# A four-stage mixture-of-experts kernel: slot logits in steps of one PSUM bank, the third stage's batch end in two single banks, bias parts in later entries, and new instruction orders

## What is computed

```python
x = x + L0_ffn(L0_cond(x, cond))   # attention with gated experts, then an 8-expert MoE
x = x + L1_ffn(L1_cond(x, cond))   # one chosen expert MLP, then routed experts and a layernorm
x = x + L2_ffn(L2_cond(x, cond))   # two chosen skill MLPs and a shared one, then a soft MoE
x = x + L3_ffn(L3_cond(x, cond))   # masked linear mix, 16-head attention, shared and routed experts
```

```python
logits = (einsum('tzd,ed->tze', x, phi_w) + phi_b).reshape(t, z, n, p)
D = softmax(logits, axis=3); C = softmax(logits, axis=2)
X = clip(einsum('tznp,tzd->npd', D, x)); X = tanh(normalise(X))
Y = einsum('npd,ndH->npH', X, expert_w) + expert_b
out = einsum('tznp,npH->tzH', C, Y)
```

## Time and profile before

| | us |
|---|---|
| median of 3 runs | 1338.59 (1337.62 to 1344.19) |
| profiled execution | 1348.07 |
| its span, first to last instruction | 1346.3 |
| TensorE busy in it | 1107.3 |
| VectorE busy | 749.8 |
| ScalarE busy | 448.1 |
| GpSimd busy | 176.7 |
| mean granted TensorE clock | 0.897 of full speed |

### The profile page before, as it was taken

How to read it: one execution, slowest core, us unless ns; L and a number is a source line. 1 busy time by engine, 2 the same in 40 slices (tenths; PEclk the granted TensorE clock), 3 DMA queues, 4 the chain that set the end, 5 groups by cost and what they waited for, 6 DMA issues and landing times.

```text
span 1346.3 us, 17637 instructions
## 1 busy us (share of the span) xinstructions
PE 1107.3 (82%) x6726; PEld 784.2 (58%) x6726; DVE 749.8 (56%) x1645; ACT 448.1 (33%) x712; POOL 176.7 (13%) x170
## 2 busy tenths in 40 slices
PE   1358999999758999999898866579889898898775
PEld 0247888888645566567565434456556565665543
DVE  3245555655373556766666775264574755747533
ACT  1113545443441323343233211214333343333231
POOL 0982001110010000000000100112020120201100
PEclk8578999999877989999999886789999999999887
DMA  9000000000020121012100000300000000000000
GB/s 317 1 1 1 13 13 13 13 13 13 1 94 0 47 110 48 1 47 110 48 0 1 0 0 1 95 1 1 5 1 5 0 5 5 1 5 1 4 5 4
DMA packets 12890, 35.21 MB, mean 26 GB/s; under 512 B 3552, under 2 KB 7296, under 8 KB 12035
## 3 DMA queue, kind: packets, MB, share of 16 engines
q1 hardware_dynamic: 12486, 32.63, 6.9%
q10 hardware_dynamic: 288, 1.44, 0.3%
q0 software_dynamic: 32, 0.01, 0.0%
HBM read 33.02 MB, written 1.05 MB: 25 GB/s over the span
## 4 chain that ended last, share of the span: by engine, by line
PE 56%; issue 16%; DVE 13%; POOLq 4%; DVEq 4%; ACT 3%; POOL 2%; SPq 1%; DMA 1%; ACTq 0%
PE ps L1079 5%; PE ps L983 4%; PE ps L1009 4%; PE ps L1213 3%; PE ps L961 3%; PE ps L798 3%; PE ps L954 3%; PE ps L946 3%; PE ps L1067 3%; PE ps L808 2%; PE ps L1140 2%; DVE arena L1867 2%; PE ps L1156 2%; PE ps L844 2%; PE ps L832 1%
## 5 line engine op out<-in xcount | busy, mean ns | idle before, releaser
L1867 DVE TENSOR_REDUCE arena<-ps 128x8 f32<-128x2048 f32 x32 | 73.2, 2288 | 31.9 <-PE ps L1120 31.7
L1418 ACT ACTIVATE arena<-ps 128x2048 f32<-128x2048 f32 x32 | 60.1, 1879 | 84.0 <-PE ps L1144 84.0
L983 PE MATMUL ps<-arena,uR 128*128 128x512 f32 x128 | 76.8, 684 | 4.7 <-ACT arena L1364 4.7
L1009 PE MATMUL ps<-arena 128*128 128x128 f32 x512 | 70.9, 296 | 11.8 <-DVE xacc L1789 8.1
L1009 PEld LDWEIGHTS ps<-arena 128*128 128x128 f32 x512 | 66.1, 208 | 19.0 <-DVE xacc L1789 10.7
L1067 PE MATMUL ps<-uR,arena 128*128 128x256 f32 x256 | 74.5, 387 | 0.7 <-ACT arena L1391 0.7
L1079 PE MATMUL ps<-arena 128*128 128x256 f32 x256 | 63.5, 397 | 5.2 <-DVE arena L1848 3.7
L1213 PE MATMUL ps<-arena 128*128 128x512 f32 x128 | 62.4, 632 | 3.4 <-DVE yT L1934 2.0
L1391 ACT ACTIVATE arena<-ps 128x512 f32<-128x512 f32 x64 | 38.3, 598 | 75.5 <-PE ps L1068 66.5
L798 PE MATMUL ps<-arena 128*128 128x256 f32 x256 | 59.7, 392 | 2.6 <-DVE arena L1616 2.6
L954 PE MATMUL ps<-x2R,arena 128*128 128x256 f32 x192 | 54.0, 404 | 9.3 <-DVE arena L1757 9.1
(11 more groups left out here) (372 smaller groups left out, 2325.1 us busy)
## 6 DMA issues: line engine op xcount, KB each, us to landing
arena<-in_skills SPq DMA_DIRECT2D x16, 768.0 KB, 5.7
arena<-in_expert_w SPq DMA_DIRECT2D x2, 2048.0 KB, 8.0
arena<-in_l_experts SPq DMA_DIRECT2D x8, 386.5 KB, 3.2
arena<-in_consts_b ACTq DMA_DIRECT2D x1, 1408.0 KB, 8.3
x2R<-in_x SPq DMA_DIRECT2D x8, 128.0 KB, 2.5
arena<-in_L_w SPq DMA_DIRECT2D x2, 512.0 KB, 8.9
arena<-in_phiC SPq DMA_DIRECT2D x1, 1024.0 KB
arena<-in_expert_b SPq DMA_DIRECT2D x1, 1024.0 KB, 5.0
```

The lines of the kernel that those rows point to most:

```text
L983: mm(o, uR[:, b, k * P:(k + 1) * P], phiC[:, col:col + 512], start=True, stop=False)
L1009: last = mm(high[:, 2, t * P:(t + 1) * P], eD[h][:, k, col:col + P], uT[u][:, k, :], start=k == 0, stop=k == 1)
L1418: av(pexp[:, t, gp].rearrange("p c h t -> p (c h t)"), scores[:, :, :].rearrange("p c t -> p (c t)"), ACT.Exp, scale=SCALE3).then_inc(s.sc ...
L1867: V.tensor_reduce(nm[:, k, :, 2 * gp:2 * gp + 2], scores[:, :, :].rearrange("p c (h t) -> p c h t", h=2), X, ALU.max, negate=True).then_in ...
```

## The change

1. Each slot step covers one bank: 8 steps in place of 4 for LG, MT and SH on TensorE, ScalarE and (LG) VectorE. Step n+1 has its own bank; only step n+2 waits for the exponential of step n. The parts of the maxima have two buffers, padded to the same transposition. The sum, inverse and scaling on VectorE and XT stay at four.
2. In the third stage AV0 to G3 use bank 2 alone, and FF to OUT use bank 3 alone. AV0 waits for the gate read (G3A) of the batch before and no longer for its output. AV1 waits for AV0's copy; AVT and SA are two steps each; FF and FH four; RT and RM four.
3. PH is three steps (PHA, PHB, PHC) with the same three operations, and they, PX, W and WA stand later in GpSimd's list.
4. All lists are written anew.

```diff
-    PH.0 RA0.0 PH.1 PX.0 RG0.0 PH.2 PH.3 W.0 WA.0 RA0.1 W.1 WA.1 W.2 WA.2 W.3 WA.3 RG0.1 W.4 WA.4 W.5 WA.5 W.6
+    RA0.0 RG0.0 RA0.1 RG0.1 PHA.0 PHB.0 PHC.0 PHA.1 PHB.1 RA0.2 PHC.1 RA1.0 PHA.2 PHB.2 PHC.2 PHA.3 PHB.3 RG1.0
+    PHC.3 W.0 RG0.2 WA.0 PX.0 W.1 RA1.1 WA.1 W.2 WA.2 RA0.3 RG1.1 W.3 WA.3 W.4 WA.4 W.5 WA.5 W.6 RG0.3 WA.6 W.7
...
-    MT0.5 SG1.7 SH0.5 SU1.7 SG2.7 SU2.7 LG1.5 SG3.7 SG4.7 MT1.5 SG5.7 SH1.5 SU3.7 SU4.7 LG2.5 XT0.5 MT2.5 SU5.7
-    SH2.5 XT1.5 LG3.5 UC.7 MT3.5 CL2.0 SH3.5 CL3.0 MC.5 CL4.0 LG0.6 CL5.0 XT2.5 CL6.0 MT0.6 CL7.0 XT3.5 SH0.6
+    SU4.7 LG4.6 MT3.6 SU5.7 SH3.6 MT4.6 LG5.6 SH4.6 UC.7 MT5.6 LG6.6 SH5.6 UT.7 XT0.6 MT6.6 LG7.6 SH6.6 CL2.0
+    LG0.7 XT1.6 MT7.6 CL3.0 MC.6 SH7.6 CL4.0 MT0.7 CL5.0 LG1.7 SH0.7 CL6.0 LG2.7 CL7.0 MT1.7 XT2.6 SH1.7 MT2.7
...
-    TS1.7 RT1.6 TS2.7 TS3.7 OUT.6 AV0.7 AV1.7 AVT.7 SAT.7 WO.7 X5T.7 G3.7 FF0.7 FF1.7 SO.7 RT0.7 RT1.7 OUT.7""",
+    TS2.7 AV0.7 OUT.5 TS3.7 FF0.6 AV1.7 FF1.6 AVT0.7 AVT1.7 FF2.6 SAT.7 WO.7 FF3.6 SO.6 RT0.6 X5T.7 RT1.6 G3.7
+    RT2.6 RT3.6 OUT.6 FF0.7 FF1.7 FF2.7 FF3.7 SO.7 RT0.7 RT1.7 RT2.7 RT3.7 OUT.7""",
```

The slot steps on TensorE:

```diff
-                        else:
-                            pe.wait_ge(s.eD_ready, at(b, 4, st_ - 1))
-                        for c in range(2):
-                            o = high[:, c, :]
-                            col = h * HALF + c * 512
-                            mm(o, uR[:, b, k * P:(k + 1) * P], phiC[:, col:col + 512], start=True, stop=False)
-                            last = mm(o, con("ones3"), phib3[:, col:col + 512], start=False, stop=True)
-                        last.then_inc(s.lg_mm, 1)
+                        else:
+                            pe.wait_ge(s.eD_ready, at(b, 8, st_ - 2))
+                        col = h * HALF + c * 512
+                        mm(high[:, c, :], uR[:, b, k * P:(k + 1) * P], phiC[:, col:col + 512], start=True, stop=False)
+                        mm(high[:, c, :], con("ones3"), phib3[:, col:col + 512], start=False, stop=True).then_inc(s.lg_mm, 1)
```

The waits and steps of the third stage's batch end on TensorE:

```diff
                         if b > 0:
-                            pe.wait_ge(s.out_ready, at(b - 1))
+                            pe.wait_ge(s.g3_read, at(b - 1))
+                    else:
+                        pe.wait_ge(s.av_read, at(b, 2, 0))
...
-                if n in ("FF0", "FF1"):
...
+                for q in range(4):
+                    if n == f"FF{q}":
+                        v, j = q // 2, q % 2
+                        if q == 0:
+                            pe.wait_ge(s.x5C_ready, at(b))
+                            if b > 0:
+                                pe.wait_ge(s.out_ready, at(b - 1))
+                        else:
+                            pe.wait_ge(s.ffh_ready, at(b, 4, q - 1))
+                        w = (wsi, w1s)[v]
+                        mm(low[:, 3, 0:T], w[:, j, :], x5C[:, :], start=True, stop=True)
+                        mm(low[:, 3, T:2 * T], w[:, 2 + j, :], x5C[:, :], start=True, stop=True).then_inc(s.ff_mm, 1)
...
+                for r in range(4):
+                    if n == f"RT{r}":
+                        k, c = r // 2, r % 2
+                        if r == 0:
+                            pe.wait_ge(s.y2_ready, at(b))
+                        else:
+                            pe.wait_ge(s.rt_read, at(b, 4, r - 1))
```

More of the change, by code:

```diff
@@ L149 @@
+    PHC.3 W.0 RG0.2 WA.0 PX.0 W.1 RA1.1 WA.1 W.2 WA.2 RA0.3 RG1.1 W.3 WA.3 W.4 WA.4 W.5 WA.5 W.6 RG0.3 WA.6 W.7
+    WA.7 RA0.4 RA1.2 RG0.4 RG1.2 RA1.3 RA0.5 RG1.3 RG0.5 RA0.6 RA1.4 RG1.4 RG0.6 RA1.5 RA0.7 RG1.5 RG0.7 RA1.6
+    RG1.6 RA1.7 RG1.7""",
 }
@@ L540, in build @@
         phib_h = w3y[0:3].rearrange("p b d -> p (b d)")[:, 0:HALF // 2].bitcast(BF16)
-        nmd = tb([P, 32])
-        nmd3 = tb([P, P], BF16)
-        mdT = tb([64, P], BF16)
+        nmd = tb([P, 16])
+        nmd3 = [tb([P, P], BF16) for _ in range(2)]
+        mdT = [tb([64, P], BF16) for _ in range(2)]
         dsum = tb([P, 32])
-        nmc = tb([P, K, 2, 32])
+        nmc = tb([P, K, 4, 32])
+        mcn = tb([P, K, 32])
         mc3 = tb([P, K, P], BF16)
@@ L968, in step_b @@
                     last.then_inc(s.uC_T, 1)
-                for st_ in range(4):
-                    h, k = st_ // 2, st_ % 2
+                for st_ in range(8):
+                    h, k, c = st_ // 4, st_ // 2 % 2, st_ % 2
                     if n == f"LG{st_}":
-                        if st_ == 0:
+                        if st_ < 2:
                             pe.wait_ge(s.uC_ready, at(b))
@@ L991, in step_b @@
                     if n == f"SH{st_}":
-                        pe.wait_ge(s.mdT_ready, at(b, 4, st_))
-                        pe.wait_ge(s.lg_read, at(b, 4, st_))
-                        for c in range(2):
-                            last = mm(high[:, c, :], mdT, selD[:, c * 512:(c + 1) * 512],
-                                      start=False, stop=True, skip_group_check=True)
-                        last.then_inc(s.lg_shift, 1)
+                        pe.wait_ge(s.mdT_ready, at(b, 8, st_))
@@ L998, in step_b @@
+                        pe.wait_ge(s.lg_read, at(b, 8, st_))
+                        mm(high[:, c, :], mdT[c], selD[:, 0:512], start=False, stop=True,
+                           skip_group_check=True).then_inc(s.lg_shift, 1)
                 for q in range(4):
@@ L1212, in step_d @@
                         for j in range(2):
-                            last = mm(low[:, 2 + c, :], pm[:, 2 + j, k * P:(k + 1) * P],
-                                      w2e[:, j, c * 512:(c + 1) * 512], start=j == 0, stop=j == 1)
-                    last.then_inc(s.rt_mm, 1)
+                            last = mm(low[:, 3, :], pm[:, 2 + j, k * P:(k + 1) * P], w2e[:, j, c * 512:(c + 1) * 512],
+                                      start=j == 0, stop=j == 1)
+                        last.then_inc(s.rt_mm, 1)
@@ L1218, in step_d @@
                     for k in range(K):
[L1219 removed]
+                        last = tr(low[:, 3, k * P:(k + 1) * P], finT[:, k, :], ident)
                     last.then_inc(s.fin_T, 1)
@@ L2017, in _ @@
             pool.wait_ge(s.a_done, 1)
-            G.memset(nmd3, 0.0)
+            for c in range(2):
+                G.memset(nmd3[c], 0.0)
             G.memset(mc3, 0.0)
```

382 lines of the change are left out of this document (196 added, 186 removed).

## The result

The changed kernel takes 1256.92 us (median of 4 runs, 1254.30 to 1258.35) against 1338.32 for the kernel before beside it: ratio 0.937 (0.934 to 0.941). The prediction was 1287, range 1256 to 1321. The direction was right; the gain was 81 us where 52 were forecast. The profiled execution took 1257.37 us for a span of 1255.5, so it stands at its median, while the profiled one of before (1348.07) stood some 10 us above its own.

What follows compares the result with a forecast made beforehand. TensorE was taken as the bound within the three stages, with the remaining loss at the seams; -18 - 20 - 14 = -52 from 1338.6 gave 1287 us, range 1256 to 1321 for 8 in 10.

Steps and rivals of the forecast that it cites:

- Part 1: First stage: moving GpSimd's bias to later entries starts the gate chain sooner; -18 us, ends -28 and -8.
- I let this eat the entry 1 gain whole: First stage: delays from moved GpSimd work, 2 to 3 us per operation, cancel the gain from entry 1's removed stall.
- Part 2: Second stage: slot logits in eight one-bank steps with new orders; -20 us, ends -38 and 0.
- 5 x 9 = 45 against 8 x 10.4 = 83: -38: Second stage's tail after UC.7: 10 half steps, worth 5 at 9 us, replace 8 whole steps at 10.4; -38 us.
- the term +18: Second stage: three slot steps moved ahead of UC.7 cost TensorE 6 us each there, with only 22 idle us.
- With one bank each, two half steps stand in turn: Second stage: a pair of half steps costs the larger of VectorE's 7.3 us and TensorE's share; taken as 9.
- Part 3: Third stage: the batch's end in two single banks, overlapping the next batch's attention; -14 us, ends -30 and +5.
- half of 31 idle us, -15: Steady third stage: filler steps win about half of TensorE's 31 idle us in 330; -15 us.
- The very end: Kernel's end: batch 6's end moves behind batch 7's attention, and batch 7's last rounds run alone; +1 us net.
- All far ends: Rival, whole kernel: all three changes reach their far gains, -96 us, half the excess counted; about 1265 us, chance 0.14.
- VectorE's queue becomes the bound: Rival, second stage: TensorE waits for VectorE's more, smaller steps, so only the start gains; 1318 us, chance 0.16.
- exposed table loads: Rival, second and third stage: 52 more ScalarE table loads all delay the chain, +67 us; 1354 us, chance 0.07.

Runs made afterwards that it cites:

- with the weight sums spread: Changed kernel with GpSimd's eight weight-sum pairs placed one each behind a gate power of entries 3 to 6: 1254.36 us against 1256.92.
- in the old order: Kernel before with eight one-bank slot steps, the two halves side by side where each whole step stood: 1358.52 us against 1338.22.
- part 3's kernel: Kernel before with only the batch's end in two single banks and the new third-stage orders: 1315.78 us against 1337.45.
- the run with 95 more: Changed kernel with a one-column silu ahead of each of 64 slot exponentials, adding 95 table loads: 1328.72 us against 1256.92.
- both bank splits: Kernel before with single banks but old step places, separately for slot steps and the batch's end: ratios 1.013 and 1.066.

## Why the prediction was right and wrong, by its steps

**Part 1, forecast -18 (ends -28 and -8), measured -7.** The dates at the start were right to 1.3 us (27.99 for 28.1, 43.7 for 45), and so was 0 for the other engines' orders, as far as the times tell. The step that failed is "I let this eat the entry 1 gain whole". The moved GpSimd work took more than that. I had the symptom in the earlier trace rows (2.15 us for a 0.59 us operation) but priced it as single operations standing in front, 2 to 3 us. In fact several operations of one chain are each held until the one of GpSimd beside them ends, 5.6 us in one gate chain, with a TensorE wait of 7.9. That is a part of the missing 11 us: with the weight sums spread, BC came 3 to 5 us forward. For the rest I can only argue. TensorE is the bound in the rest of this stage (148 of 160 us busy), so a sooner start was worth only the work done in the gaps. The profiles put BC at 391.1 to 393.0 with the new first stage and at 403.6 to 404.6 in four of five with the old one, more than the 7 us of the times; where the difference goes stays open.

**Part 2, forecast -20 (ends -38 and 0), measured -49, the largest miss.** The tail was right: "5 x 9 = 45 against 8 x 10.4 = 83: -38" came as -38 to -41, and its distances as 8.2 and 10.7. What failed is the term +18, "The three steps moved ahead of UC.7 cost TensorE 6 each there ... since it has only 22 idle us". That stretch became 5 to 6 us *shorter* (10.8 against the profiled execution of before). Two things were wrong in it. The 6 us are a sum of overlapping durations; in the windows 88 or 89 more matmuls raised TensorE's busy time by 10.5 to 11.2 us, not 18. And the idle time counted as a reserve that stays, where the new order took 16 of 27.5 us out of it, with the clock up from 0.96 to 0.97. So even the end "if the moved steps fill idle time", -38, was too tight; it left no room for the stretch itself to gain. These two stretches make some 44 of the 49 us; the rest is within what single executions differ by.

The reason I gave for the gain was also only half of one. "With one bank each, two half steps stand in turn" does nothing by itself: in the old order a pair takes 10.8 us where I had put 9, and the kernel loses 17 to 20 us. Single banks permit the order that has the effect.

**Part 3, forecast -14 (ends -30 and +5), measured -22 to -24.** The mechanism held, and the sizes did not. The term "half of 31 idle us, -15" should have been nearly all: 7 us are left in 300, which is 23 of the 31. The very end was forecast at +1 net and is 109 us behind the last S in place of 94.6, with 9.5 us more busy and 5 us more idle time. Batch 5's routed products now stand behind the last S (from 1164 in the changed kernel), so the sum is safer taken from JX to the end, first before and then part 3's kernel:

```profile
853.40:1346.30 492.90, 418.86 (x3204) 276.65 (x3204) 267.35 (x426) 164.72 (x258) 59.87 (x54) 0.93 0.02 7
844.80:1314.10 469.30, 412.99 (x3204) 272.55 (x3204) 263.71 (x474) 189.71 (x292) 60.27 (x54) 0.93 0.02 7
```

The same number of matmuls, 23.6 us less: 17.7 of them are idle time (74.0 to 56.3) and 5.9 busy time.

**The rivals.** "All far ends", 1265, came nearest, and that is luck: it had part 1 at its far end of -28, and part 1 gave 7; part 2 gave 49, beyond its own far end of -38. Of "VectorE's queue becomes the bound" the mechanism is real (0.64 us per added us) but the half reduction cost what I took (0.69), so it did not decide. Of exposed table loads hardly any wait shows in the changed kernel, though the run with 95 more shows that the room I assumed for them is nearly used up. What the change's own loads cost is not measured, so the total does not decide between the 2.66 us a switch of the Trainium skill (page "ScalarE: Activation LUTs", section "What ACT_TABLE_LOAD costs") and my cost of 0; no drain behind a load shows here either, the operation behind it starting within 0.02 us of its end.

## What to carry over

Where a stage leaves idle time on the engine that bounds it, price a finer order as a share of all that idle time, and not by adding moved work to a stretch that is taken as full; take the work's cost from a window, not from a sum of overlapping durations. Smaller buffers by themselves only added hand-overs here: both bank splits were slower than before (1.3% and 6.6%) until the steps between the hand-overs were reordered. Keep GpSimd's large operations away from chains of small VectorE ones where TensorE waits for the chain (worth some 3 us here), and look at the last batch by itself, since buffers that its predecessors needed are free there.

## What the runs showed that I had not expected

- Four of VectorE's small operations beside GpSimd's 1.9 to 2.3 us ones ended 0.02 to 0.04 us after them: they are held, not slowed. A MAX8 beside the same operation was not held.
- A busy share is no measure of room in a queue: VectorE at 73% and ScalarE at 51% passed on 0.64 and 0.53 of each added microsecond.
- At the end of the kernel a fuller queue had TensorE's clock back sooner: at 1.00 from 1220 and no longer at 0.50 up to 1238. Batch 7's sixteen matmuls took 7.03 us in one stretch, where they had taken 3.78, 3.78, 3.65 and 1.99 us with gaps of 0.78 between.
